# Windowed attention scores computed in quadrants of 64 queries by 192 keys

## The chip, the cores and the metric

One Trainium2 chip, one of its cores. The metric is the device time of one execution of the whole kernel in microseconds, the median of several runs. The engines have separate instruction streams and are ordered only by semaphores: TensorE (PE in the profile, with its weight loads as PEld), VectorE (DVE), ScalarE (ACT), GpSimd (POOL) and SyncE (SP), which issues the DMA transfers.

## The reference, cut to what matters

The whole program is a mixture of experts with an attention over segments, then a hyperbolic attention block, and at the end two layers of windowed attention with a gated feed-forward. The change touches only those two last layers. There are 8 sequences of 512 tokens, 8 heads of 64 dimensions, all in float32. A window is 128 tokens, and a query sees the window before its own and its own:

```python
bq = q.reshape(b, h, w, WINDOW, d) * QK_SCALE          # WINDOW = 128, d = 64
bk, bv = look_around(bk), look_around(bv)              # window before, own window
sim = jnp.einsum('bhwid,bhwjd->bhwij', bq, bk)         # 128 queries x 256 keys
mask = (i < j) | (i > j + WINDOW) | (j == -1)
sim = jnp.where(mask, -jnp.finfo(sim.dtype).max, sim)
attn = jax.nn.softmax(sim, axis=-1)
out = jnp.einsum('bhwij,bhwjd->bhwid', attn, bv)
```

So query r of a window (r from 0 to 127) sees the 256 keys only from r to r + 128. The first 64 queries never see keys 192 to 255, the last 64 never see keys 0 to 63. In the first window of a sequence only the last 128 of the 256 keys exist.

## The kernel before

Everything below is in `window_layers`. 16 items (8 sequences in each of 2 layers) follow one another. An item has 4 tiles of 128 tokens (t = 0 to 3), and a tile is worked in two halves of four heads. One half of one tile is a step G, so that an item starts every U = 8 steps and the attention of all items fills steps 0 to 127. Around each step the parts of neighbouring items are laid by hand: `phase` says in which steps a part runs, and each engine's block runs the parts that are due in a fixed order.

In step G TensorE runs, in this order, the transposes of the probabilities of step G (`turned_probabilities`, line 2616, 8 matmul records, 4 where t is 0), the scores of step G + 1 (`scores`, L2631), in some steps a projection (`input_rows`, L2669) or the transposes of rotated queries and keys (`turn_heads`, L2680), then probabilities by values (`outputs_of_heads`, L2650), the output projection (L2688), more projections (L2669) and the feed-forward of an earlier item (L2696, L2707, L2718) or the transposes of new inputs (L2659).

`scores` makes four matmuls, for two pairs of heads c2 and two row groups g. The queries of head g lie in partitions 64g to 64g + 63, so the two heads of a pair use the two row halves of the array, and each writes its own PSUM bank (`ps[:, g]`). Each matmul takes 128 queries as weights and moves 256 keys, or 128 keys where t is 0 (`lo` is then 128). In float32 the profile records each as two matmuls and two weight loads; hence 8 records of L2631 a step. The transposes appear as one record each.

VectorE in step G copies half of the turned probabilities out of PSUM (L2424), adds the mask to the scores of step G + 1 and takes the row maxima (`masked_scores`, L2435 and L2440), does keys, norms, statistics or the first part of the rotation (L2470), multiplies the exponentials by the reciprocal of their sum (`probabilities`, L2448 and L2450), and ends with the second part of the rotation (`rope_two`, L2476 and L2479), normalised rows (L2522) or gated products (L2529). ScalarE takes the exponentials (L2296) and other copies. TensorE's L2616 of step G waits for L2450 of step G, L2680 for L2479, and L2650 for L2424. The mask adds -1e30 where a key is not seen, after which the exponential gives zero for it, whatever the score was, as long as it is a finite number.

`pre_ok` counts the fills at the start; GpSimd, VectorE and TensorE wait until it has reached `PRE`.

Of the kernel before, what the change touches and what calls it, by code (L numbers as in the profile page):

```python
# [15 lines left out]
P = 128  # L16
# [1980 lines left out]
def window_layers(nc, io, xs, x1, out):  # L1997
# [15 lines left out]
    with ExitStack() as ctx:  # L2013
        def sb(name, shape, dt=F32):
            return ctx.enter_context(nc.sbuf_tensor("w_" + name, shape, dt))

        def sem(name):
            return ctx.enter_context(nc.semaphore("w_" + name))
# [22 lines left out]
        qT = sb("qT", [P, NC, L])  # L2041
        kT = sb("kT", [P, NC, L])
# [22 lines left out]
        ps = ctx.enter_context(nc.psum_tensor("wps", [P, 8, 512], F32))  # L2065
# [8 lines left out]
        full = {k: sem(f"full{k}") for k in (5, 6, 7)}  # L2074
        free = {k: sem(f"free{k}") for k in (5, 6, 7)}
        pre_ok, rots_ok = sem("pre_ok"), sem("rots_ok")
        PRE = 5
        sq_ok, n2_ok, nr_ok, rope_ok = sem("sq_ok"), sem("n2_ok"), sem("nr_ok"), sem("rope_ok")
        s_mm, sm_ok, p_ok, pn_ok = sem("s_mm"), sem("sm_ok"), sem("p_ok"), sem("pn_ok")
        pT_mm, pT_a, pT_v, pv_mm, oT_ok = sem("pT_mm"), sem("pT_a"), sem("pT_v"), sem("pv_mm"), sem("oT_ok")  # L2080
# [103 lines left out]
        def emptied(eng, *job):  # L2184

            k, n = place[job]
            eng.wait_ge(free[k], n + 1)
# [69 lines left out]
        def _(pool):  # L2257
            g = nc.gpsimd
            g.memset(mhalf[:], -0.5).then_inc(pre_ok, 1)
            pool.wait_ge(pre_ok, PRE)  # L2260
            for G in STEPS:
# [135 lines left out]
        def _(dve):  # L2397
            v = nc.vector
# [2 lines left out]
            v.memset(hs[:, :, 0], 0.0).then_inc(pre_ok, 1)  # L2401
            v.memset(st[:], 0.0).then_inc(pre_ok, 1)
            v.memset(h2T[:, MH - 1], 1.0).then_inc(pre_ok, 1)
            dve.wait_ge(ld_c, 2 * 16)
            for l in range(NL):
                for s in range(2):
# [3 lines left out]
            dve.wait_ge(rots_ok, 4 * NL)  # L2410
            dve.wait_ge(pre_ok, PRE)
            dve.wait_ge(ld_s, 2 * 16)
# [182 lines left out]
        def _(pe):  # L2595
            te = nc.tensor
# [22 lines left out]
            def scores(G):  # L2619
                i, u = divmod(G, U)  # L2620
                t, half = u // 2, u % 2
                lo = P if t == 0 else 0
                if G:
                    pe.wait_ge(sm_ok, G)
                if half == 0:
                    emptied(pe, "tq", i, t)
                    emptied(pe, "tk", i, t)
                for c2 in range(2):
                    for g in range(2):
                        c = 2 * half + c2  # L2630
                        ins = te.matmul(ps[:, g, c2 * 256 + lo:c2 * 256 + 256], qT[64 * g:64 * g + 64, c, t * P:(t + 1) * P],  # L2631
                                        kT[64 * g:64 * g + 64, c, t * P - P + lo:(t + 1) * P], start=True, stop=True)
                ins.then_inc(s_mm, 1)

            def outputs_of_heads(G):
# [86 lines left out]
            pe.wait_ge(ld_s, 2 * 16)  # L2722
            pe.wait_ge(pre_ok, PRE)
            for G in STEPS:
                if attends(G):
                    turned_probabilities(G)
                if attends(G + 1):
                    scores(G + 1)
# [139 lines left out]
def program(nc, io, out):  # L2868
    x1 = nc.dram_tensor("x1", (B, L, D), F32, kind="Internal").ap() if "x1" not in io else io["x1"]
    xs = nc.dram_tensor("xs", (3 * B, L, D), F32, kind="Internal").ap() if "xs" not in io else io["xs"]  # L2870
    with ExitStack() as outer:
        ball = ball_parts(nc, io, x1, xs, outer)
        moe_attention(nc, io, x1, ball)
        ball_block(nc, ball)
    window_layers(nc, io, xs, x1, out)
# [13 lines left out]
```

## Time and profile before

| what | value |
|---|---|
| median of 3 runs | 3566.89 us (3561.45 to 3569.26) |
| the profiled execution, its own time | 3563.92 us |
| its span, first to last instruction | 3562.1 us |
| mean granted TensorE clock over the span | 0.972 |
| TensorE busy | 3319.4 us |
| VectorE busy | 2125.5 us |
| ScalarE busy | 1731.8 us |

The profiled execution is one run; its time and span differ by 1.8 us of start and end. A start time in a row counts from the first instruction. A matmul record lasts longer than the time to the next one's start, as matmuls are pipelined; what a group costs TensorE is read from its start to the start of the next group. PEclk is the share of the full TensorE clock that was granted.

### The profile page before, as it was taken

What the parts mean: (1) busy time and instruction counts of PE and PEld (TensorE: products, weight loads), DVE (VectorE), ACT (ScalarE), POOL (GpSimd) and SP (SyncE); (2) the same over time, 40 slices, a digit from 0 to 9 for tenths busy, and PEclk for the clock granted to TensorE, in tenths of its full rate; (3) what the DMA queues carried; (4) which work ended last, traced back from release to release, by engine and by line L of the source; (5) the groups of instructions that cost most, each with busy time, mean ns of one, the idle gap of its engine ahead of it and who ended that gap; (6) DMA issues with size and microseconds to landing.
All of it is one profiled execution on the core that took longest, in us unless ns stands there. A gap on an engine that the chain in (4) does not pass through costs nothing. (4 is left out here: it accounts for less than half of the span.)

```text
span 3562.1 us, 51625 instructions
## 1 busy us (share of the span) xinstructions
PE 3319.4 (93%) x18018; PEld 1923.0 (54%) x18018; DVE 2125.5 (60%) x6268; ACT 1731.8 (49%) x3299; POOL 562.1 (16%) x698
## 2 busy tenths in 40 slices
PE   8999999999997788999999658999999999999998
PEld 3455555555555434544444435566666666666665
DVE  3243343343346557677765547777777777777773
ACT  2233333333333366566555325655656666555562
POOL 0000000000002333434431211111111111111110
PEclk9999999999999799999999879999999999999999
DMA  4110111101100200000000030000000000000000
GB/s 180 54 63 30 40 37 44 63 30 39 54 13 13 82 6 11 7 16 14 11 13 13 9 138 19 18 22 22 22 25 22 22 21 28 29 28 27 22 29 20
DMA packets 77898, 120.69 MB, mean 34 GB/s; under 512 B 10222, under 2 KB 66227, under 8 KB 72520
## 3 DMA queue, kind: packets, MB, share of 16 engines
q1 hardware_dynamic: 77640, 117.38, 9.7%
q8 instruction: 145, 2.38, 0.3%
q14 instruction: 113, 0.93, 0.1%
HBM read 96.35 MB, written 16.83 MB: 32 GB/s over the span
## 5 line engine op out<-in xcount | busy, mean ns | idle before, releaser
L2669 PE MATMUL wps<-w_wqkv,w_hT 128*128 128x512 f32 x768 | 378.3, 617 | 3.1 <-DMA w_wo<-in_wwo 3.1
L2268 POOL TENSOR_TENSOR w_rn<-w_n,w_mhalf 128x16 f32<-128x16 f32 x64 | 189.2, 2956 | 1053.1 <-DVE w_n L2459 1053.1
L2707 PE MATMUL wps<-w_xnT,w_w 128*128 128x512 f32 (+1 forms) x704 | 319.6, 597 | 24.5 <-DVE w_xnT L2522 20.5
L1219 POOL TENSOR_TENSOR b_routs<-b_rins,b_expo 128x4 f32<-128x4 f32 x88 | 90.6, 1032 | 1496.1 <-DVE b_rins L1439 1496.1
L2296 ACT ACTIVATE w_pr<-w_sm,w_nmx,w_rn 128x256 f32<-128x256 f32 (+1 forms) x512 | 286.6, 562 | 9.1 <-DVE w_nmx L2440 8.4
L656 PE MATMUL ps<-xT,b_late 128*128 128x512 f32 x512 | 245.8, 603 | 0.0
L672 PE MATMUL ps<-hid,b_late 128*128 128x512 f32 x512 | 240.8, 593 | 0.0
L2707 PEld LDWEIGHTS wps<-w_xnT,w_w 128*128 128x128 f32 (+1 forms) x704 | 132.1, 190 | 188.5 <-issue 164.8
L1284 ACT ACTIVATE bb_pr<-ps 128x1024 f32<-128x1024 f32 x128 | 130.4, 1018 | 180.0 <-PE ps L1814 179.6
L2669 PEld LDWEIGHTS wps<-w_wqkv,w_hT 128*128 128x128 f32 x768 | 137.9, 193 | 131.9 <-issue 126.9
L298 ACT ACTIVATE hid<-ps,rb 128x512 f32<-128x512 f32 x128 | 87.9, 687 | 223.2 <-PE ps L656 223.0
L2283 ACT ACTIVATE w_pT<-wps 128x512 f32<-128x512 f32 (+1 forms) x128 | 69.6, 544 | 249.2 <-PE wps L2616 249.2
L2435 DVE CUSTOM_DVE_ANT_0 w_sm<-wps,w_wmask 128x256 f32<-128x256 f32 (+1 forms) x512 | 168.8, 385 | 20.9 <-issue 20.6
L2718 PE MATMUL wps<-w_w,w_h2T 128*128 128x256 f32 x768 | 170.9, 380 | 3.3 <-issue 3.3
L2718 PEld LDWEIGHTS wps<-w_w,w_h2T 128*128 128x128 f32 x768 | 145.9, 190 | 35.6 <-issue 17.5
L672 PEld LDWEIGHTS ps<-hid,b_late 128*128 128x128 f32 x512 | 97.3, 190 | 121.7 <-issue 121.3
L2305 ACT ACTIVATE w_qkr<-wps 128x512 f32<-128x512 f32 x128 | 76.1, 595 | 156.3 <-PE wps L2669 155.9
L510 DVE TENSOR_REDUCE mx<-ps 128x8 f32<-128x512 f32 x32 | 22.1, 691 | 217.1 <-PE ps L753 217.1
L1897 PE MATMUL ps<-bb_uT,bb_wf 128*128 128x512 f32 x256 | 121.3, 614 | 23.9 <-DVE bb_fT L1671 14.5
L407 DVE TENSOR_TENSOR hid<-hid,wm 128x512 f32<-128x512 f32 x128 | 88.3, 690 | 88.1 <-ACT hid L298 87.1
L2616 PEld LDWEIGHTS wps<-w_ident,w_pr 128*128 128x128 f32 x896 | 105.2, 142 | 65.8 <-issue 38.2
L2450 DVE TENSOR_SCALAR w_pr<-w_pr,w_ri 128x256 f32<-128x256 f32 (+1 forms) x512 | 137.6, 333 | 4.5
(333 smaller groups left out, 6804.1 us busy)
## 6 DMA issues: line engine op xcount, KB each, us to landing
b_late<-in_ew SPq DMA_DIRECT2D x32, 1024.0 KB, 6.8
w_xa<-xs SPq DMA_DIRECT2D x16, 512.0 KB, 3.9
w_xin<-xs SPq DMA_DIRECT2D x64, 128.0 KB, 4.2
xT<-in_xT SPq DMA_DIRECT2D x8, 512.0 KB, 3.8
xres<-in_x SPq DMA_DIRECT2D x32, 128.0 KB, 2.2
x<-x1t SPq DMA_DIRECT2D x32, 128.0 KB, 1.7
b_mod<-ada SPq DMA_DIRECT2D x16, 256.0 KB, 3.2
xs<-bb_wb SPq DMA_DIRECT2D x8, 512.0 KB, 2.8
```

The costliest lines, as they stand in the source:

```text
L656: ins = te.matmul(ps[:, G % 2], w1[:, k, j % M1 * P:(j % M1 + 1) * P], xT[:, b % 2, k], start=(k == 0), stop=(k == KD - 1))
L672: ins = te.matmul(ps[:, 2 + c], w2[:, j % M1, c * P:(c + 1) * P], hid[:, G % 4], start=(j == 0), stop=(j == J - 1))
L1284: a.activation(pr[:, G % 2, 0:2], ps[:, SC:SC + 2], ACT.Exp, scale=DH ** -0.5).then_inc(p_ok, 1)
L1897: ins = te.matmul(to, wf1[:, k, m * P:(m + 1) * P], uT2[:, k], start=(k == 0), stop=(k == KD - 1))
L2268: g.tensor_tensor(rn[:, i % 2, t], n2[:, n % 2, 1], mhalf[:], ALU.pow).then_inc(nr_ok, 1)
L2296: ins = a.activation(pr[:, j, lo:], sm[:, j, lo:], ACT.Exp, bias=nmx[:, G % 2, j:j + 1], scale=rn[:, i % 2, t, h:h + 1], accum_out=rs[:, G ...
L2435: ins = v.tensor_tensor_reduce(out=sm[:, j, lo:], in0=ps[:, g, c2 * 256 + lo:c2 * 256 + 256], in1=wmask[:, lo:], scale=1.0, scalar=-3.0e38 ...
L2450: ins = v.tensor_scalar(pr[:, j, lo:], pr[:, j, lo:], ri[:, G % 2, j:j + 1], None, ALU.mult)
L2616: ins = te.transpose(ps[:, 2 + g, (2 * c2 + k) * P:(2 * c2 + k + 1) * P], pr[:, j, k * P:(k + 1) * P], ident[:])
L2669: ins = te.matmul(to, hT[:, i % 2, k, t * P:(t + 1) * P], wqkv[:, i // B, k, s * 512:(s + 1) * 512], start=(k == 0), stop=(k == KD - 1))
L2707: ins = te.matmul(to[0:n], w1[:, i // B, k, lo:lo + n], xnT[:, k], start=(k == 0), stop=(k == KD - 1))
L2718: ins = te.matmul(to[:, a * D:(a + 1) * D], h2T[:, m, t * P:(t + 1) * P], w2[:, i // B, m], start=(m == 0), stop=(m == MH - 1))
```

## The change

Each matmul of the scores is cut in two by queries: q = 0 takes the first 64 queries of the tile and writes partitions 0 to 63, q = 1 the last 64 and writes partitions 64 to 127. Both use 64 rows and 64 columns of the array, so a pair of heads now makes four matmuls of 64 by 64. Each moves only the keys that its queries can see: 0 to 191 for q = 0 and 64 to 255 for q = 1; where t is 0, 128 to 191 and 128 to 255. The rest of the two PSUM banks is never written by a matmul, and VectorE still reads it, so it is filled with zeros once at the start, which makes one more count of `pre_ok`.

```diff
--- before.py
+++ after.py
@@ -2074,7 +2074,7 @@
         full = {k: sem(f"full{k}") for k in (5, 6, 7)}
         free = {k: sem(f"free{k}") for k in (5, 6, 7)}
         pre_ok, rots_ok = sem("pre_ok"), sem("rots_ok")
-        PRE = 5
+        PRE = 6
         sq_ok, n2_ok, nr_ok, rope_ok = sem("sq_ok"), sem("n2_ok"), sem("nr_ok"), sem("rope_ok")
         s_mm, sm_ok, p_ok, pn_ok = sem("s_mm"), sem("sm_ok"), sem("p_ok"), sem("pn_ok")
         pT_mm, pT_a, pT_v, pv_mm, oT_ok = sem("pT_mm"), sem("pT_a"), sem("pT_v"), sem("pv_mm"), sem("oT_ok")
@@ -2401,6 +2401,7 @@
             v.memset(hs[:, :, 0], 0.0).then_inc(pre_ok, 1)
             v.memset(st[:], 0.0).then_inc(pre_ok, 1)
             v.memset(h2T[:, MH - 1], 1.0).then_inc(pre_ok, 1)
+            v.memset(ps[:, 0:2], 0.0).then_inc(pre_ok, 1)
             dve.wait_ge(ld_c, 2 * 16)
             for l in range(NL):
                 for s in range(2):
@@ -2626,10 +2627,13 @@
                     emptied(pe, "tq", i, t)
                     emptied(pe, "tk", i, t)
                 for c2 in range(2):
-                    for g in range(2):
-                        c = 2 * half + c2
-                        ins = te.matmul(ps[:, g, c2 * 256 + lo:c2 * 256 + 256], qT[64 * g:64 * g + 64, c, t * P:(t + 1) * P],
-                                        kT[64 * g:64 * g + 64, c, t * P - P + lo:(t + 1) * P], start=True, stop=True)
+                    c = 2 * half + c2
+                    for q in range(2):
+                        k0, k1 = max(lo, 64 * q), 192 + 64 * q
+                        for g in range(2):
+                            ins = te.matmul(ps[64 * q:64 * q + 64, g, c2 * 256 + k0:c2 * 256 + k1],
+                                            qT[64 * g:64 * g + 64, c, t * P + 64 * q:t * P + 64 * q + 64],
+                                            kT[64 * g:64 * g + 64, c, t * P - P + k0:t * P - P + k1], start=True, stop=True)
                 ins.then_inc(s_mm, 1)
 
             def outputs_of_heads(G):
```

## Rows read from the trace of the kernel before

**Rows 1.** The page of the profile: busy time of the engines, then the span in 40 slices.

```profile
PE 3319.4 (93%) x18018; PEld 1923.0 (54%) x18018; DVE 2125.5 (60%) x6268; ACT 1731.8 (49%) x3299; POOL 562.1 (16%) x698
...
PE   8999999999997788999999658999999999999998
...
PEclk9999999999999799999999879999999999999999
```

**Rows 2.** Stretches: busy time of each engine, granted clock, DMA share, GB/s.

```profile
2166.50:2208.50 42.00, 37.13 (x236) 23.71 (x236) 36.11 (x115) 23.94 (x60) 7.57 (x3) 1.00 0.04 10
2518.60:3307.60 789.00, 776.75 (x4069) 491.21 (x4068) 586.91 (x1835) 475.78 (x1008) 119.49 (x45) 1.00 0.08 25
3466.00:3495.00 29.00, 23.99 (x135) 14.34 (x133) 15.70 (x64) 15.38 (x34) 0.00 (x0) 0.94 0.10 30
```

**Rows 3.** Waits of TensorE between 2500 and 3100 us, all of them.

```profile
PE wps L2707 <- DVE w_xnT L2522: 9.5, 7, 1.4
```

**Rows 4.** Groups of TensorE instructions by line and shape: busy us, mean ns of one.

```profile
L2631 PE MATMUL wps<-w_kT,w_qT 64*128 64x256 f32 x768 | 110.3, 406 | 0.0
...
L2631 PE MATMUL wps<-w_kT,w_qT 64*128 64x128 f32 x256 | 22.9, 297 | 0.0
```

**Rows 5.** TensorE in order of time, steps 64 and 65: start us, us.

```profile
2814.06 0.72 PE L2631 MATMUL wps<-w_kT,w_qT 64*128 64x128 f32 x8
2814.71 1.99 PE L2669 MATMUL wps<-w_wqkv,w_hT 128*128 128x512 f32 x4
...
2822.15 1.13 PE L2631 MATMUL wps<-w_kT,w_qT 64*128 64x256 f32 x8
2823.22 1.09 PE L2680 MATMUL wps<-w_ident,w_qk 128*128 128x128 f32 x8
2824.24 0.66 PE L2650 MATMUL wps<-w_pT,w_vt 128*64 128x128 f32 x8
```

**Rows 6.** TensorE in order of time, in the kernel's first part.

```profile
244.37 0.60 PE L809 MATMUL ps<-b_ident,att 128*128 128x128 f32 x4
244.90 0.70 PE L753 MATMUL ps<-kT,qT 64*64 64x64 f32 x32
245.52 1.56 PE L656 MATMUL ps<-xT,sw 128*128 128x512 f32 x3
```

**Rows 7.** VectorE in order of time, steps 60, 64 and 65.

```profile
2771.07 0.42 DVE L2435 CUSTOM_DVE_ANT_0 w_sm<-wps,w_wmask 128x256 f32<-128x256 f32 x1 [0.39 <-issue]
...
2813.74 0.75 DVE L2529 SCALAR_TENSOR_TENSOR w_h2T<-wps,w_b,w_gl 128x512 f32<-128x512 f32 x1 [0.97 <-PE wps L2707]
...
2814.84 0.29 DVE L2435 CUSTOM_DVE_ANT_0 w_sm<-wps,w_wmask 128x128 f32<-128x128 f32 x1
...
2821.59 1.23 DVE L2479 TENSOR_TENSOR w_qk<-w_qk,w_t 128x1024 f32<-128x1024 f32 x1
...
2823.33 0.41 DVE L2424 COPY w_pT<-wps 128x256 f32<-128x256 f32 x1
```

**Rows 8.** TensorE in order of time, step 5.

```profile
2183.50 1.09 PE L2616 MATMUL wps<-w_ident,w_pr 128*128 128x128 f32 x8 [1.47 <-DVE w_pr L2450]
...
2185.96 1.09 PE L2680 MATMUL wps<-w_ident,w_qk 128*128 128x128 f32 x8 [0.30 <-DVE w_qk L2479]
```

**Rows 9.** VectorE in order of time, step 5.

```profile
2184.68 1.22 DVE L2479 TENSOR_TENSOR w_qk<-w_qk,w_t 128x1024 f32<-128x1024 f32 x1
...
2186.44 0.42 DVE L2435 CUSTOM_DVE_ANT_0 w_sm<-wps,w_wmask 128x256 f32<-128x256 f32 x1
```

**Rows 10.** VectorE where the last two layers begin.

```profile
2095.24 0.48 DVE L2403 MEMSET w_h2T<- 128x512 f32 x1
2099.03 0.43 DVE L2407 SCALAR_TENSOR_TENSOR w_rots<-w_h2T,w_qks 128x256 f32<-128x256 f32 x1 [3.30 <-DMA w_qks<-in_qks]
```

**Rows 11.** TensorE where the last two layers begin.

```profile
2101.72 1.94 PE L2659 MATMUL wps<-w_ident,w_xa 128*128 128x128 f32 x8 [22.09 <-DMA w_xa<-xs]
```

**Rows 12.** TensorE in the last steps with attention.

```profile
3457.64 1.09 PE L2650 MATMUL wps<-w_pT,w_vt 128*64 128x128 f32 x16 [0.66 <-DVE w_pT L2424]
```

## The prediction

> **What bounds the kernel now.** I read the page first: TensorE is busy 93% of the span, VectorE 60%, and in the slices of the last two layers (from about the 25th on) TensorE stands at nine tenths with the full clock granted [rows 1]. Then stretches of those layers. In the steady part, 9 items in 789 us or 87.7 us an item, TensorE is busy 776.75 us, 98.4%, at a granted clock of 1.00, while VectorE is busy 74% and ScalarE 60%. In the filling part (2166 to 2208 us) TensorE is busy 88% and VectorE 86%; near the end (3466 to 3495 us) TensorE is down to 83% [rows 2]. The waits of TensorE in 600 steady us are only seven, 1.36 us each, all L2707 for the normalised rows [rows 3]. So in the steady part time taken off TensorE's queue is time off the kernel, as long as no slack on VectorE runs out; while the layers fill and empty it must be checked step by step. The groups by shape give what is at stake: the scores hold TensorE busy 110.3 and 22.9 us [rows 4].
>
> **The new burst.** A burst is counted from its start to the start of the next group. With 256 keys it takes 2823.22 - 2822.15 = 1.07 us, with 128 keys 2814.71 - 2814.06 = 0.65 us [rows 5]. Each has four rounds (two pairs of heads, two records for a float32 matmul) in which both row halves work together. 4 x 128 columns more cost 0.42 us, so a column costs 0.82 ns and the rest of a burst is 1.07 - 4 x 256 x 0.82 ns = 0.23 us, the change of tiling and first weights included.
>
> The first part of the kernel holds the very form that the change makes: L753, 64 rows by 64 columns, two row halves by two column halves, each row half with a PSUM bank of its own. 32 records go from 244.90 to 245.52, in 0.62 us [rows 6]. If four work at once these are 8 rounds of 64 columns, 8 x 64 x 0.82 = 0.42 us, and the rest is 0.20 us, about that of the bursts above. If they worked in pairs, the streaming alone would take 0.84 us, more than was measured. Four at once it is, at least with 64 columns. The way in is a change from 128*128 too (L809), as it will be from L2616, and there is one change in and one out before and after.
>
> With 192 keys the new burst has four rounds: 4 x 192 x 0.82 = 0.63 us, and a rest. I take 0.20 us as in L753, so 0.83 us against 1.07, **0.24 us saved**. The rest can be 0.23 as in the old burst (0.21 saved), or 0.18, since L753 has 8 rounds of four starts and this has four (0.26 saved). Where t is 0, a round is as long as its longer tile, 128 columns, as before: 0.42 + 0.20 = 0.62 us against 0.65, **0.03 us saved** (0 to 0.05); the 64 columns of the other tile save nothing.
>
> At this place a rule of the Trainium skill speaks against the change. The rows charge L753 at most 0.20 us beside the streaming for 32 records, 6 ns each. TensorEngine Tiling, Instruction Overhead, says that every matmul on TRN2 carries about 60 cycles of overhead, and that one shouldn't cut a size that is already small. As an estimate from that page, at 2.4 GHz, 25 ns for each of 8 more records would take back 0.20 us of every burst: 0.04 us saved in long ones, 0.17 us lost in short ones.
>
> **What is unchanged or hidden.** VectorE reads the same 256 columns with the same instructions; the cells that are never written hold zero. The fill of 128x1024 is new. The one of 128x512 before it takes 0.48 us, and VectorE then stands 3.30 us until a transfer has landed [rows 10]; TensorE's first work waits for its input and comes at 2101.72 us, after an idle 22.09 us [rows 11]. Between once and three times 0.48 us for each 512 columns gives 1 to 3 us, which fits in the 3.30 us. I cost it at nothing; without that cover it would be these 1 to 3 us once. The higher count of `pre_ok` holds TensorE and GpSimd no longer than this.
>
> **Does the time saved reach the end?** The scores of step n + 1 are made in step n. Of the 128 bursts 96 are long and 32 short; all of it would be 96 x 0.24 + 32 x 0.03 = 24.0 us. Two things can keep it: a wait of TensorE for VectorE, behind a chain that didn't start earlier, or one that is new.
>
> *Steady.* The only wait there, L2707's, ends a chain that begins at the scores: in step 60 VectorE's L2435 begins after an idle 0.39 us [rows 7], so it waits for them and has 0.39 - 0.24 = 0.15 us over. All behind it moves with the scores. The tightest place is step 65. VectorE is behind there from 2813.74 us, when L2707 releases it, on: in step 64 L2435 begins at 2814.84 with hardly any idle, and the rotation's last part ends at 2821.59 + 1.23 = 2822.82 us; TensorE wants it for L2680 at 2823.22 [rows 5, 7], 0.40 us later. TensorE will be there earlier by the short burst of step 64 and the long one of step 65, 0.03 + 0.24 = 0.27 us, and 0.06 us go by between an end and the start that it releases (in step 5 L2479 ends at 2185.90 and L2680 starts at 2185.96 [rows 8, 9]). 0.07 us are left: no wait, but only just. Next on VectorE is the copy L2424, over at 2823.74, wanted by L2650 at 2824.24 [rows 5, 7]: 0.50 us, of which 0.27 goes. At the other steps of an item both are wider. From step 13 to 120 there are 80 long and 28 short bursts: 80 x 0.24 + 28 x 0.03 = 20.0 us.
>
> *Filling, steps 0 to 12.* In odd steps VectorE bounds: in step 5 TensorE waits 0.30 us for L2479 right after the scores [rows 8] and L2435 follows with no idle time [rows 9], long after the scores are there. The time saved becomes a longer wait of L2680. In the even steps L2435 does wait for the scores, as in step 60. Five long bursts count (steps 2, 4, 6, 10, 12): 1.2 us.
>
> *Emptying, from step 121.* In step 123 L2650 waits 0.66 us for the copy L2424, behind the scores [rows 12], and steps 121, 122 and 124 wait in the same way; only the scores of steps 125 and 126 begin chains that are waited for. 0.4 us of 1.4 counts.
>
> The sum is 20.0 + 1.2 + 0.4 = **21.6 us**. Against the profiled execution's own time, 3563.92 us, that is 3542.3. That execution lies 3 us under the median of the runs shown, inside their spread of 7.8 us; from the median it would be 3545.3. I say **3542 us**, 0.6 to 0.7% faster. A difference under 0.2%, 7 us here, couldn't be told from none.
>
> **The rivals.**
> *VectorE keeps part.* If the margin of 0.07 us in step 65 isn't there, because the burst saves 0.26 us or the release takes longer, TensorE waits for L2479 in one step of each item; if the chain behind it (L2424, L2435) is also held, a second burst is lost. 14 items x 0.24 us is 3.4 us, twice that 6.7 us: 3546 to 3549 us. For it: the small margin. Against: VectorE has 26% idle, so it can't go on. Chance 0.12.
> *A price for each record.* If the 0.62 us of L753 is all issuing, 19 ns for each of 32 records, and only hidden streaming beside it, the price could come on top here: 0.63 + 16 x 0.019 = 0.93 us, 0.14 saved in a long burst, and 0.42 + 0.31 = 0.73, 0.08 lost in a short one: 96 x 0.14 - 32 x 0.08 = 10.9 us, 3553 us. Against it: the old bursts, with 8 records, have a rest of 0.23, not less than L753's with 32. Chance 0.05. By the page's 60 cycles it would be 96 x 0.04 - 32 x 0.17 = -1.6 us, 3565 us and no change; since L753 shows 19 ns a record with everything in it, I give this a chance of 0.03.
> *Slower: the quadrants go in pairs.* The two quadrants of a row half read different keys from the same 64 partitions. If these reads share one path when they are long, a long burst has 8 rounds, 8 x 192 x 0.82 + 0.20 = 1.46 us, 0.39 more than now, and a short one 4 x (64 + 128) x 0.82 + 0.20 = 0.83 us, 0.18 more: 96 x 0.39 + 32 x 0.18 = 43 us, 3607 us. It decides as soon as a round of 192 columns takes (1.07 - 0.20) / 4 = 0.218 us instead of 0.157, 1.4 times its streaming. For it only that no row has more than 64 columns in this form; against it that L753 reads two different pieces from the same partitions too, at full speed. Chance 0.05.
> *It is hidden anyway.* Then something other than TensorE would have to bound the steady part; 98.4% busy with one wait an item says no. Chance 0.02, 3564 us.
>
> **How the numbers follow.** The forecast has 0.73, VectorE's part 0.12, prices of records 0.05 and 0.03, hidden 0.02, pairs 0.05. The forecast's own range: with 0.26 and 0.05 us a burst the sum is 80 x 0.26 + 28 x 0.05 + 5 x 0.26 + 0.4 = 23.9 us, from the fastest run 3561.5 - 23.9 = 3537.6, and I put 3536, since some of the 2.4 us counted as lost may be kept; with 0.21 and nothing it is 18.3 us, from the median 3548.6. With VectorE's part and the dearer records it becomes 3536 to 3553. Faster by over 0.2% has 0.73 + 0.12 + 0.05, less 0.01 for an unlucky set of runs: 0.89; within it 0.03 + 0.02 + 0.01 = 0.06; slower 0.05.
>
> **What the profile after would show.** L2631 has 2048 records of form 64*64, and from its start to the next group's 0.83 us where t is above 0 (0.81 to 0.86 fit) and 0.62 where it is 0. An item takes 87.7 - 6 x 0.24 - 2 x 0.03 = 86.2 us in the steady part, TensorE stays over 98% busy and its waits there are still one of 1.4 us an item; a second one, for L2479, once an item, is the first rival. L2680's wait in step 5 grows from 0.30 to 0.54 us, L2650's in step 123 from 0.66 to 0.90. The prediction is wrong if the burst takes over 0.9 us, if a new wait appears in the steady part, or if the granted clock there is no longer 1.00.

## The result and the profile after

The changed kernel took 3540.32 us (median of 4 runs, 3538.03 to 3541.27) against 3567.82 us before: a ratio of 0.9925, 95% interval 0.9908 to 0.9943. Run once more beside the old kernel it took 3541.94 us against 3565.72 us, 0.9937 (0.9924 to 0.9951). The two profiled executions took 3563.92 us and 3540.04 us, 23.9 us apart; the sum had said 21.6.

The page of the profile shows the same picture as before [rows 1]: TensorE sets the pace, a little shorter, at the same clock. Below it stand two stretches: first a long piece of the steady part, then exactly one item, from L2617 of step 61 to L2617 of step 69 (columns as in [rows 2]).

```profile
PE 3292.7 (93%) x19042; PEld 1899.5 (54%) x19042; DVE 2126.6 (60%) x6269; ACT 1732.2 (49%) x3299; POOL 562.3 (16%) x698
...
PE   7999999999998788998899758999999999999998
...
PEclk8999999999999799999999879999999999999999
```

```profile
2508.00:2762.00 254.00, 249.90 (x1522) 157.43 (x1521) 190.64 (x599) 155.20 (x327) 39.80 (x15) 1.00 0.08 23
2771.38:2857.45 86.07, 84.70 (x518) 53.28 (x516) 64.74 (x203) 52.89 (x112) 12.86 (x5) 1.00 0.07 22
```

An item takes 86.07 us instead of 87.67, TensorE is busy 84.70 of them, 98.4% as before. The line numbers have moved: L2616 is now L2617, the scores L2631 are now L2634, L2650 is L2654, L2680 is L2684, L2707 is L2711, and on VectorE L2424 is L2425, L2435 is L2436, L2479 is L2480. The waits of TensorE between 2500 and 3100 us, all of them, are those of [rows 3]:

```profile
PE wps L2711 <- DVE w_xnT L2523: 9.6, 7, 1.4
```

The scores by shape (as [rows 4]), then TensorE in order of time in steps 61, 64 and 65 (as [rows 5]):

```profile
L2634 PE MATMUL wps<-w_kT,w_qT 64*64 64x192 f32 x1536 | 84.8, 336 | 0.0
...
L2634 PE MATMUL wps<-w_kT,w_qT 64*64 64x128 f32 x256 | 20.9, 282 | 0.0
...
L2634 PE MATMUL wps<-w_kT,w_qT 64*64 64x64 f32 x256 | 14.3, 230 | 0.0
```

```profile
2772.35 0.88 PE L2634 MATMUL wps<-w_kT,w_qT 64*64 64x192 f32 x16
2773.16 1.09 PE L2684 MATMUL wps<-w_ident,w_qk 128*128 128x128 f32 x8
...
2803.28 0.67 PE L2634 MATMUL wps<-w_kT,w_qT 64*64 64x64 f32 x16
2803.88 1.98 PE L2673 MATMUL wps<-w_wqkv,w_hT 128*128 128x512 f32 x4
...
2811.32 0.88 PE L2634 MATMUL wps<-w_kT,w_qT 64*64 64x192 f32 x16
2812.14 1.09 PE L2684 MATMUL wps<-w_ident,w_qk 128*128 128x128 f32 x8
```

From start to next start a long burst (256 keys before, 192 now) takes 2773.16 - 2772.35 = 0.81 us (1.07 before), a short one (where t is 0) 0.60 (0.65 before). Single rows are rounded; averaged over the scores of steps 14 to 120 a long burst takes 0.811 us (1.065 before) and a short one 0.598 (0.645). So 0.254 us are saved in a long burst and 0.047 in a short one. VectorE in steps 60 and 65 (as [rows 7]):

```profile
2760.86 0.42 DVE L2436 CUSTOM_DVE_ANT_0 w_sm<-wps,w_wmask 128x256 f32<-128x256 f32 x1 [0.16 <-issue]
...
2810.77 1.22 DVE L2480 TENSOR_TENSOR w_qk<-w_qk,w_t 128x1024 f32<-128x1024 f32 x1
```

In step 60 VectorE still has an idle 0.16 us before the scores arrive (0.39 before). In step 65 L2480 ends at 2811.99 and L2684 starts at 2812.14, 0.15 us later. 0.06 us pass between an end and the start that it releases, so this is no wait.

The start of the last two layers, VectorE and then TensorE (as [rows 10, 11]):

```profile
2095.72 0.91 DVE L2404 MEMSET wps<- 128x1024 f32 x1 [0.21 <-issue]
2098.81 0.43 DVE L2408 SCALAR_TENSOR_TENSOR w_rots<-w_h2T,w_qks 128x256 f32<-128x256 f32 x1 [2.18 <-DMA w_qks<-in_qks]
```

```profile
2101.82 1.94 PE L2663 MATMUL wps<-w_ident,w_xa 128*128 128x128 f32 x8 [22.41 <-DMA w_xa<-xs]
```

The fill took 0.91 us and VectorE still waited 2.18 us for its transfer. And TensorE's waits in steps 5 and 123 (as [rows 8, 12]), both longer by the time that the scores lost, 0.30 to 0.56 and 0.66 to 0.91 us:

```profile
2184.18 0.98 PE L2684 MATMUL wps<-w_ident,w_qk 128*128 128x128 f32 x7 [0.56 <-DVE w_qk L2480]
...
3435.56 1.09 PE L2654 MATMUL wps<-w_pT,w_vt 128*64 128x128 f32 x16 [0.91 <-DVE w_pT L2425]
```

### The profile page after: what moved, and what is told of

Its sections match the earlier page's. It is cut to its first block and busy times, and to the rows that moved or that the text cites. A ratio compares the mean times of both kernels' runs of the same rounds, so it can differ in the third digit from the quotient of the medians.

```text
span 3538.3 us, 53674 instructions
## 1 busy us (share of the span) xinstructions
PE 3292.7 (93%) x19042; PEld 1899.5 (54%) x19042; DVE 2126.6 (60%) x6269; ACT 1732.2 (49%) x3299; POOL 562.3 (16%) x698
## 5 line engine op out<-in xcount | busy, mean ns | idle before, releaser
L2711 PE MATMUL wps<-w_xnT,w_w 128*128 128x512 f32 (+1 forms) x704 | 319.8, 597 | 24.6 <-DVE w_xnT L2523 20.6
L2711 PEld LDWEIGHTS wps<-w_xnT,w_w 128*128 128x128 f32 (+1 forms) x704 | 131.8, 189 | 189.1 <-issue 165.2
L2436 DVE CUSTOM_DVE_ANT_0 w_sm<-wps,w_wmask 128x256 f32<-128x256 f32 (+1 forms) x512 | 168.8, 385 | 8.3 <-issue 8.3
L2617 PEld LDWEIGHTS wps<-w_ident,w_pr 128*128 128x128 f32 x896 | 104.4, 141 | 65.9 <-issue 38.5
```

Source lines behind the costliest of these rows:

```text
L2436: ins = v.tensor_tensor_reduce(out=sm[:, j, lo:], in0=ps[:, g, c2 * 256 + lo:c2 * 256 + 256], in1=wmask[:, lo:], scale=1.0, scalar=-3.0e38 ...
L2617: ins = te.transpose(ps[:, 2 + g, (2 * c2 + k) * P:(2 * c2 + k + 1) * P], pr[:, j, k * P:(k + 1) * P], ident[:])
L2711: ins = te.matmul(to[0:n], w1[:, i // B, k, lo:lo + n], xnT[:, k], start=(k == 0), stop=(k == KD - 1))
```

## The experiments

All start from the changed kernel. The theory is that of the prediction: TensorE's queue is what bounds the steady part, and a burst costs its rounds times the columns of a round, four quadrants (64 by 64 tiles) at once, plus a small rest. Each ratio is to the kernel before, run beside.

**All keys again.** Only the range of the keys is undone.

```diff
-                        k0, k1 = max(lo, 64 * q), 192 + 64 * q
+                        k0, k1 = lo, 256
```

> Quadrants of 64 by 64, but each moves all the keys again (256, or 128 where t is 0). My theory: a burst is 4 rounds x columns x 0.82 ns plus the rest that the changed kernel shows, 0.81 - 4 x 192 x 0.82 ns = 0.18 us, so long bursts take 1.02 us and short ones stay at 0.60. An item in the steady part takes 86.07 + 6 x 0.21 = 87.3 us, the kernel about 3540 + 20 = 3560 us, so that most of the gain is the columns and some 6 us (0.05 us in each of 128 bursts) come with the smaller weight loads. Rival, the gain is in the tiling and not in the columns: bursts stay near 0.81 us and the kernel at 3540. Rival, reads of two pieces from the same partitions share a path when they are long: a round of 256 columns takes well over 0.21 us and the kernel is slower than 3567.

Measured: 3560.51 us, a ratio to the kernel before of 0.9984 (0.9974 to 0.9994). TensorE in order of time, one long burst and what follows:

```profile
2782.22 1.09 PE L2634 MATMUL wps<-w_kT,w_qT 64*64 64x256 f32 x16
2783.25 1.10 PE L2684 MATMUL wps<-w_ident,w_qk 128*128 128x128 f32 x8
```

1.03 us a burst, 1.025 on average, and 87.34 us an item. So 0.21 of the 0.25 us saved are the 64 columns that are no longer moved, and 0.04 us come with the smaller tiles at equal columns. Reads of two pieces from the same partitions don't hinder one another, even with 256 columns.

Where the 0.04 us lie can be seen in the records of one burst, first of the kernel before, then of this run (ns: shortest, median, longest):

```profile
L2631 PE MATMUL wps<-w_kT,w_qT x8: 376/376/480, 2822.2 to 2822.9; 64*128 64x256 f32 x8
...
L2634 PE MATMUL wps<-w_kT,w_qT x16: 376/376/427, 2782.2 to 2782.9; 64*64 64x256 f32 x16
```

The longest are those of the first round, and the second round starts later by the same amount: 0.10 us extra with 128 columns of weights, 0.05 with 64. Of the 0.05 between them the two additional starts in a round, 7 ns apart, take back 0.01.

**Another order.** The loops over pairs and halves of queries change places, so that the matmuls on the first two quadrants stand ahead of those on the other two.

```diff
-                for c2 in range(2):
-                    c = 2 * half + c2
-                    for q in range(2):
-                        k0, k1 = max(lo, 64 * q), 192 + 64 * q
+                for q in range(2):
+                    k0, k1 = max(lo, 64 * q), 192 + 64 * q
+                    for c2 in range(2):
+                        c = 2 * half + c2
                         for g in range(2):
```

> The same matmuls as in the changed kernel in another order: both pairs of heads with the first 64 queries, then both with the last 64, so that neighbours in the queue are no longer on four different quadrants. My theory, four at once is what pays: the two quadrants of a row half now follow one another, 7 or 8 rounds of 192 columns instead of 4, a long burst of 7 x 0.157 + 0.2 = 1.30 to 8 x 0.157 + 0.2 = 1.46 us, a short one about 0.83 us, and the kernel at 3540 + 96 x (0.49 to 0.65) + 32 x 0.2 = 3593 to 3609 us, slower than before the change. Rival, the queue finds the free quadrants by itself whatever the order: burst 0.81 us and 3540 us. Rival, the order costs but little because records are bound by something other than streaming: under 1.0 us a burst, under 3560 us.

Measured: 3544.80 us, 0.9944 (0.9927 to 0.9962), 86.16 us an item. TensorE in order of time, then the scores' instructions alone in four short stretches of that burst (in brackets how many records are under way):

```profile
2775.76 0.90 PE L2634 MATMUL wps<-w_kT,w_qT 64*64 64x192 f32 x16
2776.59 1.10 PE L2684 MATMUL wps<-w_ident,w_qk 128*128 128x128 f32 x8
```

```profile
2775.77:2775.79 0.02, 0.02 (x2) 0.02 (x2) 1.00 0.00 0
2775.79:2775.83 0.04, 0.04 (x4) 0.04 (x6) 1.00 0.00 0
2775.86:2775.96 0.10, 0.10 (x4) 0.10 (x8) 1.00 0.00 0
```

My theory of this run fell; the first rival was right. The burst takes 0.83 us, not 1.30. Four records are under way within 0.07 us of the burst's start, while the first eight records of the program's order all need the same two quadrants, whose next turn comes only when 192 columns, 0.16 us, have gone by. So the third and the fourth must be of the other two quadrants, started ahead of their place.

A short burst shows it directly, as its two halves have different lengths: the first half of the queries moves 64 keys, the second 128, and in this run's order eight records of 64 columns stand ahead of the first of 128. What TensorE had under way in the burst's first 0.06 us:

```profile
L2634 PE MATMUL wps<-w_kT,w_qT 64*64 64x128 f32 x2 | 0.3, 320 | 0.0
L2634 PE MATMUL wps<-w_kT,w_qT 64*64 64x64 f32 x2 | 0.3, 267 | 0.0
```

Two records of 128 columns have started, six of 64 that stand ahead of them have not. This takes the queue's order to be that of the program; the trace doesn't number the instructions. The other rival, records bound by something other than streaming, fits the 0.83 us as well, but not the run before, in which 64 more columns cost 0.21 us. The order costs 0.014 us a burst, no more.

**Twice the records.** Each matmul is cut in two by its keys.

```diff
-                    for q in range(2):
-                        k0, k1 = max(lo, 64 * q), 192 + 64 * q
-                        for g in range(2):
+                    for part in range(2):
+                        for q in range(2):
+                            k0, k1 = max(lo, 64 * q), 192 + 64 * q
+                            km = (k0 + k1) // 2
+                            a, b = (k0, km) if part == 0 else (km, k1)
+                            for g in range(2):
...
-                            ins = te.matmul(ps[64 * q:64 * q + 64, g, c2 * 256 + k0:c2 * 256 + k1],
+                                ins = te.matmul(ps[64 * q:64 * q + 64, g, c2 * 256 + a:c2 * 256 + b],
```

> Every matmul of the scores is cut once more, into two halves of its keys (96 and 96 columns): 32 records a burst instead of 16, the same columns. My theory, the record itself costs little beside its streaming: 8 rounds, 0.63 + 0.20 = 0.83 us a long burst, 0.62 a short one, the kernel at 3540 + 128 x 0.02 = 3543 us. Rival, each record has a price of its own: at the 19 ns of L753 16 x 0.019 = 0.30 us a burst more, 3540 + 39 = 3579 us. By the 60 cycles of the Trainium skill's page TensorEngine Tiling (an estimate of 25 ns at 2.4 GHz) it would be 0.40 us a burst more and 3591 us.

Measured: 3544.34 us, 0.9946 (0.9928 to 0.9964), 86.17 us an item.

```profile
2773.46 0.89 PE L2637 MATMUL wps<-w_kT,w_qT 64*64 64x96 f32 x32
2774.28 1.09 PE L2687 MATMUL wps<-w_ident,w_qk 128*128 128x128 f32 x8
```

32 records take 0.82 us where 16 took 0.81. 16 more cost 0.01 us in long bursts (0.03 in short ones, 0.625 us instead of 0.598): not 19 ns each and not 25.

**Time put back.** The first two matmuls of probabilities by values are done twice.

```diff
-                for c2 in range(2):
+                for pad, c2, k in [(1, 0, k0)] + [(0, c2, k) for c2 in range(2) for k in range(k0, 2)]:
                     c = 2 * half + c2
-                    for k in range(k0, 2):
...
-                                            pT[:, g, c2, k], start=(k == k0), stop=(k == 1))
+                                            pT[:, g, c2, k], start=(k == k0), stop=bool(pad or k == 1))
```

> The changed kernel with TensorE time put back: the first two matmuls of probabilities by values are done twice in each step (4 records, 2 rounds of 128 columns, 2 x 128 x 0.82 = 0.21 us), after the scores have been handed over as early as in the changed kernel. My theory, the steady part is bound by TensorE's queue: 0.21 us in each of 8 steps takes 1.68 us of the 1.61 us an item that the change saved; an item takes 87.75 us and the kernel about 3540 + 23 to 27 = 3563 to 3567 us, no better than before the change. Rival, what counts is that VectorE gets the scores earlier: then the extra work is hidden, an item stays near 86.1 us and the kernel at 3540 to 3545.

Measured: 3564.13 us, 0.9994 (0.9984 to 1.0003), 87.58 us an item. TensorE in order of time, and its waits between 2500 and 3100 us:

```profile
2787.53 1.31 PE L2654 MATMUL wps<-w_pT,w_vt 128*64 128x128 f32 x20
2788.77 1.99 PE L2692 MATMUL wps<-w_wo,w_oT 128*128 128x256 f32 x8
```

```profile
PE wps L2711 <- DVE w_xnT L2523: 8.0, 7, 1.1
```

L2654 takes 1.24 us instead of 1.03. The additions are in each of an item's eight steps, and seven of them count in full; the one ahead of L2711's wait shortens that wait from 1.37 to 1.15 us. With the scores handed over just as early, the gain is gone: it was TensorE's time, not VectorE's earlier start.

**128 keys.** Each half tile of queries gets only the last 128 of its keys; the other scores are left out and read as zero.

```diff
-                        k0, k1 = max(lo, 64 * q), 192 + 64 * q
+                        k0, k1 = max(lo, 64 + 64 * q), 192 + 64 * q
```

> Each half tile of queries gets only the last 128 of its 192 keys (where t is 0 nothing changes), so part of the scores is left out and reads as zero. Long bursts become like the short ones, 0.60 us, another 0.21 us saved. My theory has VectorE take part of it from here: in step 65 of the changed kernel L2480 ends 0.15 us before L2684 starts, 0.06 is the least, so 0.09 of 0.21 us can be taken and L2684 waits some 0.12 us anew in one step of each item; and in step 60 L2436 has 0.16 us of idle time left before it, so L2711's wait grows from 1.37 to about 1.42 us. An item saves 6 x 0.21 - 0.12 - 0.05 = 1.1 us more, 84.97 us, and the kernel takes about 3524 us. Rival, TensorE alone: 6 x 0.21 = 1.26 us an item, no new wait, 3520 us. Rival, VectorE is at its end already: under 0.6 us an item, over 3531 us.

Measured: 3530.33 us, 0.9900 (0.9884 to 0.9917), 84.90 us an item. TensorE in order of time in step 65, and VectorE's work that L2684 needs:

```profile
2811.67 0.67 PE L2634 MATMUL wps<-w_kT,w_qT 64*64 64x128 f32 x16
2812.39 1.09 PE L2684 MATMUL wps<-w_ident,w_qk 128*128 128x128 f32 x8
```

```profile
2811.11 1.22 DVE L2480 TENSOR_TENSOR w_qk<-w_qk,w_t 128x1024 f32<-128x1024 f32 x1
```

An item was expected at 84.97. Elsewhere the burst takes 0.60 us to the next start, here 0.72: L2480 ends at 2812.33, L2684 starts 0.06 us later. The missing 0.12 us are VectorE's, as expected. The list of waits doesn't show them, as the burst's last record runs on until 2812.34 and leaves only 0.05 us idle. The other wait expected here, L2711's growing to 1.42 us, didn't come; it stayed at 1.36. In step 60 L2436 starts 0.74 us after the scores (2760.89 to 2761.63) where it was 0.96 in the changed kernel (2759.90 to 2760.86), so it kept all of the 0.21 us. The idle 0.16 us had been too small a measure of the margin: here L2436 starts 0.06 us before the record of the copy ahead of it ends. The kernel's time fell by 10 to 12 us rather than the 16 expected. In the profiled executions 7 us of it are lost before step 0, which TensorE reached at 2147.9 us here and at 2141.0 in the changed kernel, in a part that is the same code. Why the medians too fell by less than expected stays open.

**Strips of 32 queries.** Four strips, each with the 160 keys that it can see, zeros elsewhere as before.

```diff
-                    for q in range(2):
-                        k0, k1 = max(lo, 64 * q), 192 + 64 * q
+                    for q in range(4):
+                        k0, k1 = max(lo, 32 * q), 160 + 32 * q
                         for g in range(2):
-                            ins = te.matmul(ps[64 * q:64 * q + 64, g, c2 * 256 + k0:c2 * 256 + k1],
-                                            qT[64 * g:64 * g + 64, c, t * P + 64 * q:t * P + 64 * q + 64],
+                            ins = te.matmul(ps[32 * q:32 * q + 32, g, c2 * 256 + k0:c2 * 256 + k1],
+                                            qT[64 * g:64 * g + 64, c, t * P + 32 * q:t * P + 32 * q + 32],
```

> One step further in the same direction: strips of 32 queries, each with the 160 keys that it can see, tiles of 64 rows by 32 columns, 8 at once, 32 records a burst; the zeros filled in at the start cover the rest. My theory: 4 rounds of 160 columns, 4 x 160 x 0.82 = 0.52 us, and a rest of 0.18 to 0.25 us since a round has 8 starts 7 ns apart and weights of 32 columns: 0.70 to 0.77 us, 0.04 to 0.11 less than now; short bursts as now (their longest strip still has 128 columns), up to 0.04 more. That is 96 x 0.075 = 7 us less, less about 1 us where VectorE's margin in step 65 runs out: 3534 us (3530 to 3541). Rival, 8 tiles are not worked at once or starts don't fit into a round: bursts of over 0.9 us and over 3550 us. Rival, nothing changes, 3540.

Measured: 3535.20 us, 0.9920 (0.9904 to 0.9937), 85.43 us an item.

```profile
2762.46 0.77 PE L2634 MATMUL wps<-w_kT,w_qT 64*32 64x160 f32 x32
2763.16 1.09 PE L2684 MATMUL wps<-w_ident,w_qk 128*128 128x128 f32 x8
```

A long burst takes 0.70 us, a short one 0.60: eight tiles at once, 4 x 160 x 0.82 = 0.52 us and again a rest of 0.18. The records of that burst:

```profile
L2634 PE MATMUL wps<-w_kT,w_qT x32: 296/296/321, 2762.5 to 2762.9; 64*32 64x160 f32 x32
```

The first round's extra is now 0.025 us, with 32 columns of weights. Halving it once more gained nothing for the rest, as four more starts a round take the same time back. In step 65 the burst takes 0.72, VectorE's margin being used up.

**Both again, side by side.** The changed kernel and the strips, in more rounds.

> The changed kernel once more, beside the strips on the same chip. 3540 us again, a ratio of 0.9925 within 0.001, and 86.07 us an item in the steady part.

> The strips of 32 queries once more, beside the changed kernel. Its trace gave 85.43 us an item, 0.64 less than the changed kernel's 86.07: 16 x 0.64 = 10 us at most, some 8 us with what the filling and emptying steps keep, so 3532 us against 3540, and faster than it on this chip by 0.2%. Rival: its median of 3535 was the run-to-run change of the first part, and the two are within 3 us.

Measured: 3541.94 us, 0.9937 (0.9924 to 0.9951), for the changed kernel, 0.0002 beyond what was expected, and 3534.77 us, 0.9919 (0.9906 to 0.9933), for the strips. That is 7.2 us or 0.2% for the strips; the two intervals overlap, but in this pair the slowest run of the strips (3540.14 us) is still below the fastest of the changed kernel (3541.49), and the traces repeat within 0.01 us, 86.06 (86.07 before) and 85.43 us an item. The strips are the best version found that computes all the scores.

**More fills.** Seven more tiles of 1024 columns are filled at the start.

```diff
+            for more in (ps[:, 2:4], ps[:, 4:6], ps[:, 6:8], sm[:], xn[:], xm[:, 0], xm[:, 1]):
+                v.memset(more, 0.0).then_inc(pre_ok, 1)
```

> The changed kernel with seven more fills of 1024 columns at the start of the last two layers. In the changed kernel the one fill took 0.91 us and VectorE then still waited 2.18 us. Seven more are about 6.4 us: VectorE's wait goes to zero, 4.2 us are left, TensorE's first transposes (L2663) can't start before the last fill is over, about 1.3 us later than the 2101.8 us that their input allows, and the tables for the rotation are ready 4 us later. So the cover for a fill is real and ends between one and eight of them: L2663 begins some 7.5 us after VectorE's first fill of this part (2094.6), at 2103 us; the kernel takes 1 to 4 us more than 3540, too little to tell by time. Rival, fills are hidden whatever their number: L2663 begins 7.2 us after the first fill, as in the changed kernel. Rival, even one fill costs: then L2663 waits for VectorE already in the changed kernel, and here it begins 6.4 us later.

Measured: 3540.58 us in a single run. VectorE, then TensorE:

```profile
2095.11 0.06 DVE L2400 MEMSET w_hT<- 128x2 f32 x1 [3.27 <-PEq L1960]
...
2103.84 0.91 DVE L2406 MEMSET w_xm<- 128x1024 f32 x1 [0.16 <-issue]
```

```profile
2104.85 1.51 PE L2665 MATMUL wps<-w_ident,w_xa 128*128 128x128 f32 x6 [24.88 <-DVE w_xm L2406]
```

TensorE begins 9.74 us after VectorE's first fill, against 7.27 in the changed kernel. The expected 7.5 us didn't fit its own working: 1.3 us later than 7.27 would have been 8.6. A fill costs 1.07 us with its start, not 0.91, so seven ran 1.1 us longer still, and here they are no longer covered. One is: it is over at 2096.63, 5.2 us ahead of TensorE's first work. Most of the 2.5 us is made up again: step 0 begins 46.95 us after the first fill, against 46.48 and 46.16 in the two profiles of the changed kernel, and the time shows no loss.

## Why the prediction was right, step by step

*What bounds.* Right, and shown by the run with time put back: 0.21 us a step on TensorE brings back nearly all of the 1.6 us an item.

*The burst.* The mechanism was right, the sizes a little small. For the 0.24 us saved in a long burst 0.254 were measured, for the 0.03 in a short one 0.047, inside the stated bounds but near their end, because the rest is 0.18 us and not the 0.20 of L753. L753 has 8 rounds to this burst's 4; in the run with twice the records 4 further rounds cost 0.01 us in long and 0.03 in short bursts, which covers the 0.02 that differ. The prediction took the rest over whole from L753; it holds the first round's extra time, which goes with the columns of weights (0.10, 0.05 and 0.025 us for 128, 64 and 32), and that is why it is smaller than the 0.23 us before.

*The price of a record.* The Trainium skill's page TensorEngine Tiling (Array Packing), Instruction Overhead, gives about 60 cycles of overhead for each matmul. Added to every record, as the prediction's rival did, the traces don't agree, for neighbours on different or the same quadrants: 16 more records cost 0.01 us in all. The section also says that a matmul with a free dimension of 1 takes as long as one with 60; such a least length is tested by no run here, as every round has a tile of 64 columns or more.

*Does it reach the end.* Where TensorE stood against the kernel before, in the two profiled executions:

| stretch | predicted us | measured us |
|---|---|---|
| up to step 0 | 0 | -0.2 |
| steps 0 to 12 | 1.2 | 0.8 |
| steps 13 to 120 | 20.0 | 21.5 |
| steps 121 to 126 | 0.4 | 0.2 |
| after step 127's start | 0 | 1.6 |
| sum | 21.6 | 23.9 |

By the measured bursts the steady part is 80 x 0.254 + 28 x 0.047 = 21.6, and 21.5 were measured, so nothing is lost there. Step 65's margin held, 0.15 us where 0.13 was left by the working. By the bursts as measured it would have been 0.10; the other 0.05 came on VectorE, where L2436 of step 64 starts 1.05 us after L2530 (2802.96 to 2804.01) instead of 1.10, as the short burst hands over its scores earlier. The run with 128 keys showed both where the margin ends and that VectorE then keeps exactly what is beyond it. In steps 5 and 123 the time saved became a longer wait, as worked out.

The stretches at the two ends hold something that the prediction didn't have: the granted clock. Steps 0 to 12 and the time after step 127's start, of the kernel before, then of the changed kernel, then steps 0 to 12 of the changed kernel's second profile and the end of the run with all keys:

```profile
2140.82:2255.58 114.76, 99.01 (x568) 60.12 (x569) 93.46 (x303) 63.63 (x160) 20.19 (x8) 0.97 0.06 19
...
3495.25:3562.10 66.85, 57.25 (x208) 36.84 (x208) 18.87 (x41) 8.59 (x13) 1.01 (x1) 0.97 0.08 26
```

```profile
2141.03:2254.99 113.96, 96.27 (x673) 58.01 (x674) 93.24 (x303) 63.60 (x160) 20.24 (x8) 0.97 0.06 19
...
3473.00:3538.20 65.20, 55.61 (x208) 35.64 (x208) 18.88 (x41) 8.59 (x13) 1.01 (x1) 1.00 0.09 27
```

```profile
2143.09:2258.59 115.50, 97.48 (x673) 58.88 (x674) 93.25 (x303) 63.63 (x160) 20.19 (x8) 0.96 0.06 19
...
3492.51:3557.70 65.19, 55.61 (x208) 35.63 (x208) 18.88 (x41) 8.58 (x13) 1.01 (x1) 1.00 0.09 27
```

In the filling short pieces run at the lower of the two levels, 1.2 GHz, and not in the same steps each time. In the kernel before one slowed step 2 (9.92 us, against 8.48 in steps 4 and 6); in the changed kernel that one is missing and another slowed step 11 (9.41 against 8.51). The second profile of the changed kernel has more of them and took 0.7 us longer than the kernel before. So the 0.8 us of the table neither confirm nor refute the 1.2. Steps 4 and 6, with no such piece, each took 0.26 us less.

After step 127's start the kernel before had one short piece at the lower level (0.97 against 1.00), and none of the ten other profiles has it: nine of them, the run with all keys too, take 65.3 us there and the one with time put back 65.5, against 66.9. That is the 1.6 us of the table. As there is one profile only of the kernel before, it isn't shown whether the piece belongs to that kernel or to that execution; no mechanism of the prediction gives it. Without it the two profiled executions would be 22.3 us apart, nearer to the 21.6 of the sum.

*The 27.5 us between the first medians* are more than any trace shows. The medians of the second pair are 23.8 us apart, like the first two profiled executions. TensorE's first work of these layers began at 2101.82 us in one profile of the changed kernel and at 2103.97 in the other:

```profile
2103.97 1.94 PE L2663 MATMUL wps<-w_ident,w_xa 128*128 128x128 f32 x8 [22.18 <-DMA w_xa<-xs]
```

The first part, which is the same code, moves by microseconds from run to run; how much of the rest it explains wasn't tried.

*The rivals.* VectorE's part: not at this size, shown to begin just beyond it. A price for each record: ruled out. Quadrants in pairs: ruled out, also with 256 columns. Hidden anyway: ruled out.

## What to carry to other kernels

Where TensorE is bound by small matmuls, look for columns that no row of the result needs: cutting the output rows into tiles lets each tile move only its own columns, and the tiles work at once. Find the same form elsewhere in the trace and reckon a burst as its columns at their measured ns, plus one rest; then walk one period of the steady part and compare every slack with the time that TensorE will have gained since VectorE last waited for it. A slack, not the mean load of the other engine, says how far the next cut will pay.

## What the runs showed of the hardware that I had not expected

TensorE starts matmuls on free quadrants ahead of earlier ones that wait for theirs: with the two halves of queries in separate loops the burst took 0.83 us instead of 0.81, not 1.3 or more. Eight tiles of 64 by 32 work at once as well as four of 64 by 64: 32 records of 160 columns took 0.70 us. The first round of a burst takes longer than the later ones by 0.10 us with 128 columns of weights, 0.05 with 64 and 0.025 with 32. And cutting the float32 matmuls in two by their moving columns was nearly free, 0.01 us for 16 more records and 16 more weight loads.
